# Expert rows and normalised rows in device memory, numbered so that a partition's four rows of a chunk lie behind each other

## The reference

```
probs = softmax(x @ gate_weight.T);  top_w, top_i = top_k(probs, 2)
top_w = top_w / sum(top_w)
...
hmid = silu(g) * u;  y = einsum('enf,ehf->enh', hmid, down_proj)
out = einsum('ne,enh->nh', combine, y)
x = x + 0.5 * out
```

## Time and profile before

| | us |
|---|---|
| median of 3 runs | 1256.58 |
| lowest and highest | 1251.66, 1259.47 |
| span of the profiled execution, first to last instruction | 1263.3 |
| busy in it: TensorE, VectorE, ScalarE, GpSimd | 1066.7, 829.9, 666.1, 384.3 |
| mean granted clock of TensorE | 0.894 |

### The profile page before, as it was taken

One profiled execution on the slowest core, in us unless ns is written; L12 is line 12 of the kernel. 1 busy time (PEld: TensorE's weight loads), 2 busy tenths in 40 slices (PEclk: granted clock), 3 DMA queues, 4 the chain that ended last, 5 costly groups with the idle time before them and its releaser, 6 DMA issues. The chain is left out here.

```text
span 1263.3 us, 22520 instructions
## 1 busy us (share of the span) xinstructions
PE 1066.7 (84%) x6988; PEld 642.3 (51%) x6988; DVE 829.9 (66%) x2536; ACT 666.1 (53%) x1668; POOL 384.3 (30%) x404
## 2 busy tenths in 40 slices
PE   3539999984988899999999999999859369999940
PEld 2328888872442244443444444444347258888840
DVE  6774444436867888888888888888037754444427
ACT  5605554542753376676777666667636315455520
POOL 6506777752002000000000000000048227777730
PEclk8559999995977699999999999999889759999985
DMA  9503333326756444444444444440057113333339
GB/s 301 186 9 93 101 105 105 102 84 216 201 200 142 59 60 61 61 61 60 61 61 60 60 61 61 61 60 11 10 189 239 58 38 94 104 102 104 105 118 331
DMA packets 109248, 132.53 MB, mean 105 GB/s; under 512 B 29968, under 2 KB 83664, under 8 KB 109136
## 3 DMA queue, kind: packets, MB, share of 16 engines
q1 hardware_dynamic: 91280, 89.65, 31.2%
q0 software_dynamic: 13632, 37.24, 9.3%
q10 hardware_dynamic: 4224, 4.19, 1.0%
HBM read 82.42 MB, written 48.23 MB: 103 GB/s over the span
## 5 line engine op out<-in xcount | busy, mean ns | idle before, releaser
L1415 ACT ACTIVATE stacks_rows_or_prob<-stacks_bank 128x512 f32<-128x512 f32 (+3 forms) x768 | 326.0, 494 | 144.1 <-PE stacks_bank L1347 118.9
L1429 DVE CUSTOM_DVE_ANT_0 stacks_bank<-stacks_bank,all_causal 128x128 f32<-128x128 f32 (+3 forms) x512 | 245.4, 504 | 33.7 <-PE stacks_bank L1318 30.2
L1432 DVE TENSOR_REDUCE t_maxp<-stacks_bank 128x1 f32<-128x512 f32 x256 | 175.5, 686 | 25.0 <-PE stacks_bank L1318 24.4
L1318 PE MATMUL stacks_bank<-stacks_kst,stacks_qst 96*128 96x512 bf16 (+2 forms) x528 | 160.3, 348 | 8.5 <-DVE t_maxp L1429 4.2
L1358 PE MATMUL stacks_bank<-stacks_rows_or_prob,stacks_turned_or_values 128*32 128x512 f32 (+3 forms) x1536 | 164.5, 500 | 3.0 <-ACT stacks_rows_or_prob L1415 1.1
L1344 PE MATMUL stacks_bank<-stacks_qst,stacks_kst 99*128 99x512 bf16 (+3 forms) x528 | 154.9, 335 | 2.5 <-ACT stacks_rows_or_prob L1415 1.9
L1296 POOL COPY stacks_turned_or_values<-stacks_values 128x512 f32<-128x512 f32 x16 | 9.8, 613 | 427.7 <-DMA stacks_kst<-qk_parts 286.5
L1318 PEld LDWEIGHTS stacks_bank<-stacks_kst,stacks_qst 96*128 96x128 bf16 x528 | 48.5, 98 | 126.9 <-DVE t_maxp L1429 66.6
L653 PE MATMUL be_psG<-b_w,be_xT 128*128 x426 | 112.8, 401 | 0.0
L653 PE MATMUL ae_psG<-a_w,ae_xT 128*128 x426 | 111.9, 398 | 0.0
L1347 PE MATMUL stacks_bank<-all_causal_t,all_ident_bf 128*128 128x128 bf16 x512 | 109.6, 221 | 0.0
(11 more groups left out here) (296 smaller groups left out, 1917.7 us busy)
## 6 DMA issues: line engine op xcount, KB each, us to landing
stacks_qst<-qk_parts SPq DMA_DIRECT2D x66, 128.0 KB, 4.9
stacks_kst<-qk_parts SPq DMA_DIRECT2D x66, 128.0 KB, 7.6
stacks_rows_or_prob<-y_rows SPq DMA_DIRECT2D x16, 512.0 KB, 6.1
s_yk<-y_rows SPq DMA_DIRECT2D x16, 512.0 KB, 9.4
stacks_parts_or_stacks<-qk_parts SPq DMA_DIRECT2D x60, 128.0 KB, 6.2
qk_parts<-stacks_parts_or_stacks SPq DMA_DIRECT2D x16, 384.0 KB, 2.6
qk_parts<-q_parts SPq DMA_DIRECT2D x16, 384.0 KB, 3.4
o_rows<-t_orow SPq DMA_DIRECT2D x32, 136.0 KB, 8.7
```

The lines of the kernel that those rows point to most:

```text
L1318: nc.tensor.matmul(psR[bank][:, 0:w], qst[slot][0:KROWS, h, i * P:(i + 1) * P], kst[slot][0:KROWS, h, k0:k0 + w], start=True, stop=True).t ...
L1415: nc.scalar.activation(prob[j % 2][:, h, a:(c + 1) * 512], psS[n % ST_BANKS][:, a - c * 512:512], ACT.Exp, scale=DK ** -0.5).then_inc(exp_ ...
L1429: ins = nc.vector.tensor_tensor_reduce(psR[bank][:, 0:w], psR[bank][:, 0:w], T.causal[:, 512 - w:512], 1.0, -BIG, ALU.add, ALU.max, maxp[: ...
L1432: ins = nc.vector.tensor_reduce(maxp[:, h, col:col + 1], psR[bank][:, 0:w], AX_X, ALU.max)
```

## The change

The rows of `xn_rows` and of each half of `y_rows` are numbered anew: the token in partition p, column 4c+u, has row c*512 + 4p + u. The views of stores and loads follow that, and so does the constant with the slots' numbers, so that gathers and scatters find the same tokens under their new rows. x and the output keep their order. No instruction is added or removed.

```
-        xn_view = xn_dram.rearrange("(n p) d -> p n d", p=P)
+        xn_view = xn_dram.rearrange("(c p u) d -> p c u d", p=P, u=U)
...
-                    sp.dma_start(xn_view[:, c * U:(c + 1) * U, :], xn[:, b]).then_inc(xn_stored[b], 16)
+                    sp.dma_start(xn_view[:, c], xn[:, b]).then_inc(xn_stored[b], 16)
...
-        y_view = y_dram[0:TOPK * N, :].rearrange("(k n p) d -> p k n d", p=P, k=TOPK)
+        y_view = y_dram[0:TOPK * N, :].rearrange("(k c p u) d -> p k c u d", p=P, k=TOPK, u=U)
...
-                    sp.dma_start(yk[:, c % Y_BUFS, k], y_view[:, k, c * U:(c + 1) * U, :]).then_inc(T.y_loaded[c % Y_BUFS], 16)
+                    sp.dma_start(yk[:, c % Y_BUFS, k], y_view[:, k, c]).then_inc(T.y_loaded[c % Y_BUFS], 16)
...
-        c.link(g.iota(col_i[:], [[0, GROUPS], [P, GCOLS]], base=1, channel_multiplier=1))
+        c.link(g.iota(col_i[:], [[0, GROUPS], [U * P, GCOLS // U], [1, U]], base=1, channel_multiplier=U))
```

## The result

The changed kernel took 1247.35 us in the median of 11 runs (1242.31 to 1248.49), the kernel before 1254.76 in 11 (1247.70 to 1263.32): a ratio of 0.9928 with a 95% interval of 0.9904 to 0.9952, so 6 to 12 us are gained; the medians differ by 7.4. The prediction had 3.3 and 1253.3, with a range that began at 1248.5. The direction was right; of the size it had less than half.

The account below looks back on a forecast made before the run. The prediction took the last stage as bound by its transfers' rate, then VectorE, most of the kernel not being the DMA's to give. Last stage -3.0 and middle stage -0.3 gave -3.3 us, 1256.6 to 1253.3, range 1248.5 to 1260.

Parts of the forecast that it names:

- Rival A: Changed loads and stores: 4 KB packets gain nothing or DMA still cuts 1 KB rows; 1256.6 us within 1.5; chance 0.22.
- Rival C: Gathers and scatters: the wider row step slows them; 1257 us, or 1320 if decisive; chance 0.07, of which 0.02 decisive.
- By this row a large packet gains nothing: Lower bound from software-queue scatters and gathers: a 4 KB packet takes 207 ns, four 1 KB load packets 198.
- 392 to 400: Rate in GB/s that the prediction adopted for 4 KB packets, against 348 for loads alone and 382 beside stores.
- I take -3.0: Last stage, adding expert rows: faster loads save 3.0 us, taken between -1.7 and -5.3.
- The case that I held for the far end: Last stage: loads are served ahead of stores, no add waits, VectorE ends 5.0 us earlier; at most 5.0 + 0.3.
- 12.6 MB at 395 GB/s: Last stage: deferred stores pass the same engines, transfers take 31.9 us plus landing, so -4 or -5 at best.
- Rival B: Last stage: loads go first, VectorE never waits, output stores queue up and end the span; -1.3 us, 1255.3; chance 0.11.
- I take -0.3: Middle stage's beginning: only the first two loads are waited for, mostly in the fast burst; saves 0.2 to 0.4 us.
- The stores of normalised rows, 0: Eight stores in each of two layers: landings are covered, so no gain taken, from 0 to -0.9 us.
- the prediction's own second doubt: First stage, its DMA at 9 tenths, may be less covered than it looks, making the forecast wrong in size.
- The gathers, 0: Gathers and scatters in expert stages: only addresses change; 0 taken, from -0.5 to +1 us at each of four places.

Follow-up runs that it names:

- the crossed runs: Changed kernel with 1 KB or 4 KB packets crossed in middle-stage and last-stage loads, on one chip: means 1256.7, 1251.4, 1254.0 and 1247.2 us.
- f_44: The changed kernel itself, 4 KB packets in both stages' loads, rerun beside its padded versions on one chip: mean 1247.2 us.
- all_1k: Changed kernel with SBUF padding behind each row of all three tiles, so 1 KB packets with the new numbering: 1.0008 of the kernel before, median 1257.16 us.

## Why the prediction was right in direction and short by half

*The mechanism* was right: the DMAs went as 4 KB packets, 18,432 fewer, and with new numbering and small packets nothing was gained (1.0008 and 1.0009). Rival A falls by the 408 GB/s and the crossed runs. Rival C falls: the tile takes 2.55 us and the first gather 3.1.

*The bounds of a packet's price.* "By this row a large packet gains nothing" was rightly put aside. The upper bound, "392 to 400", was low for loads alone, 393 to 417, and nearly right for loads beside stores, 399 to 405. The 6.9% that the prediction worked out for the rate was too little for loads alone, which gained 17% (348 to 408), and about right beside stores, 5.5% (383 to 404).

*The last stage, "I take -3.0"*: this is the term that was mis-sized. The change's own worth there is -4.1 us, 39.3 in the mean of the five profiles with the old numbering and 35.3 with 4 KB packets (standard error 0.3); the crossed runs' 6 includes the gap's price of 0.9. The case that I held for the far end is the one that came: nearly all adds run without a wait (the waits behind the first fall from 4.0 to 5.4 us to 0.5 or less). I held it back with "12.6 MB at 395 GB/s" as if the transfers had still to bound the stage; they hardly do: in `f_44` the adds take 25.6 us without a gap, and the stage's 34.5 are 4.8 to the first add, these, and 4.1 for the last store. The figure of -0.2 for the first chunk, "mostly in the fast burst already", was small too: the first add comes 0.6 us earlier in the mean (4.9 us behind the issue for 5.5).

*Rival B*: its mechanism came, its price didn't. VectorE hardly waits, the output stores land 10.0 us behind their issue in the median where they took 7.1, and the end comes 4.1 to 4.8 us behind the last add and not 3.4. The landings, from the instructions of L786 in the kernel before and in the changed one:

```profile
DMA to landing us min/median/max: 3.0/7.1/8.3
```

```profile
DMA to landing us min/median/max: 4.3/10.0/14.0
```

So about 1 us of the gain was paid back, and the rest stayed, where that rival left the whole change only 1.3.

*The middle stage, "I take -0.3"*: the first adds come 0.6 us earlier (5.5 to 4.9 behind the issue). The step that may have failed is "Chunks 1 to 7 are not waited for, so their loads, and SyncE's queue behind them (the stores of q and k), give 0". It left TensorE's clock out, which was at 0.50 up to 322 us in this stage, and I read it nowhere. The stretch behind the first adds took 124.4 us in the mean with the old numbering and 121.2 with large packets, but single profiles have 119 to 133 and the difference of 3.2 has a standard error of 2.7. The crossed runs don't settle it either. Whether the packets act on the clock's rise, and how, stays open; no kernel here sets the moment of the rise by itself.

*The stores of normalised rows, 0*: the first stage may have given up to a microsecond (55.5 to 54.7 at its end, in the means), which was the prediction's own second doubt; the runs can't tell it from nothing. *The gathers, 0*, hold: 3.1 us and 2.55 a tile.

*The sum.* Shown are -4.1 in the last stage and -0.6 at the middle stage's first adds, -4.7 of the 7.4 us by the medians (9.5 by the means of the same runs, 1256.15 and 1246.67). Where the other 3 us or more come from is open; the stretch behind the first adds and the first stage are the two places that the profiles hint at. That the whole lay outside the prediction's range has thus one known cause, the last stage's term, and one that isn't.

## What to carry to other kernels

Where loads run alone and the engines wait for them, number the rows in device memory so that a partition's rows lie behind each other on both sides: the same bytes in 4 KB packets and not 1 KB ones ran at 408 GB/s for 348, and a stage that moved 12.6 MB lost 4 of its 39 us. When a stage is bound by transfers with a busy engine just behind, price the change at the point where that engine never waits, and take less only for a bound that still holds there. And read a stage's granted clock in more than one profile before pricing it: one stretch of this kernel took 119 to 133 us with the same instructions. When a control is built by padding, look whether the padding costs something by itself: here it was 0.9 us in a stage where the change was worth 4.1.

## What the runs showed of the hardware

- Loads of the same bytes by packet, running alone: 348 GB/s at 1 KB (348 to 349 in five profiles), 408 at 4 KB (393 to 417 in nine). At 2 KB, with a gap in SBUF, 395 to 403 in one profile.
- Loads of 4 KB packets beside stores of 1 KB packets: the stores' median landing went from 7.1 to 10.0 us (10.0 to 10.4 in all seven such profiles, 8.8 with 2 KB). The stores wait longer beside such loads, though bytes in all rose from 383 to 404 GB/s.
- The shortest issue of a 512 KB load on SyncE took 360 ns with rows apart in device memory, 319 with one run of 4 KB, and 517 with a gap in SBUF behind each row or each two rows. With the gap the rate fell to between 184 and 276 GB/s for a microsecond, 4 to 6 us behind a stage's first issue, in nine stages of nine.
- TensorE's granted clock rose 12 us behind the stage's first add in one run (`all_1k`) and 30 us behind it in another (the kernel before), with the same matmuls and the same gaps before it.
